# Attention with a routed expert layer on one core: another order in the prologue, slots' weights two at a time, all pieces of q and k stored between the gathers

## The reference

```python
xn  = layernorm(x)                              # no scale, no shift
q, k, v = xn @ Wq + bq, xn @ Wk + bk, xn @ Wv + bv     # 16 heads of 16
q, k = rope(q), rope(k)
att = softmax(q k^T / 4, causal) v @ Wo + bo    # per batch and head
# routed experts: 64, each token goes to 6; F = 176
w, ids = top_k(softmax(xn @ gate_w^T), 6);  w = w / (sum(w) + 1e-20)
routed = sum over the six: w * (silu(xn @ Wg_e) * (xn @ Wu_e)) @ Wd_e
shared = (silu(xn @ Sg) * (xn @ Su)) @ Sd       # width 2 * 176
out = x + att + routed + shared
```

## Time and profile before

| what | us |
|---|---|
| median of three runs | 740.29 |
| the three runs | 731.63, 740.29, 740.82 |
| the profiled execution | 730.91 |
| its span | 729.0 |
| around the span | 1.9 |
| prologue to the last tile's logits | 0 to 34 |
| projections and routing | 34 to 74 |
| shared experts | 74 to 154 |
| routed experts | 155 to 514 |
| attention | 514 to 729 |

### The profile page before, as it was taken

The page is one execution under the profiler, slowest core; times in us unless marked ns, Lnnn a source line. Parts: engine busy times, 40 slices in busy tenths (PEclk is TensorE's granted clock), DMA queues, the critical chain, the costliest instruction groups (busy, mean ns, idle before and its releaser), DMA issues.

```text
span 729.0 us, 18953 instructions
## 1 busy us (share of the span) xinstructions
PE 676.1 (93%) x4876; PEld 405.8 (56%) x4877; DVE 435.6 (60%) x1184; ACT 319.3 (44%) x830; POOL 360.6 (49%) x376
## 2 busy tenths in 40 slices
PE   7999999989999999999999999998888798899857
PEld 4745777755555555555555555554445465455534
DVE  4588999975454454454455555543557656667534
ACT  2653222224444444444444444443556445556332
POOL 3000000258587677586687878466155434554450
PEclk9999999999999999999999999999999979999879
DMA  8420001236877968869776785469865545554221
GB/s 253 136 62 0 1 1 34 85 120 198 265 218 223 308 200 270 289 199 298 233 222 210 213 255 174 100 140 326 277 195 175 166 136 170 167 173 122 75 73 44
DMA packets 77120, 124.02 MB, mean 170 GB/s; under 512 B 11047, under 2 KB 51176, under 8 KB 77080
## 3 DMA queue, kind: packets, MB, share of 16 engines
q1 hardware_dynamic: 41206, 59.89, 27.4%
q0 software_dynamic: 15872, 46.16, 21.7%
q10 hardware_dynamic: 20002, 17.47, 7.2%
HBM read 85.73 MB, written 37.75 MB: 169 GB/s over the span
## 4 chain that ended last, share of the span: by engine, by line
PE 82%; another core or an unknown queue 4%; DVE 4%; issue 3%; DMA 2%; ACT 2%; SPq 1%; DVEq 1%; ACTq 0%
PE pair L1152 22%; PE pair L1194 13%; PE pair L1138 5%; PE pair L1125 5%; PE bank L1161 4%; PE pair L1028 4%; PE pair L1176 4%; PE bank L1257 3%; PE pair L1221 3%; PE pair L1239 2%; PE bank L1289 2%; PE pair L1231 2%; PE pair L1033 2%; PE pair L1213 2%
## 5 line engine op out<-in xcount | busy, mean ns | idle before, releaser
L433 POOL DMA_INDIRECT lower<-xn_rows,idx_all x128 | 135.9, 1061 | 215.6 <-DVE idx_all L823 121.7
L1152 PE MATMUL pair<-space,work 128*64 (+1 forms) x768 | 167.0, 467 | 11.1 <-issue 4.8
L1194 PE MATMUL pair<-lower,work 88*64 x512 | 121.8, 379 | 1.3 <-ACT work L615 0.7
L833 DVE TENSOR_TENSOR work<-work,pair 128x176 f32<-128x176 f32 x160 | 53.8, 337 | 105.7 <-ACT work L600 79.7
L1152 PEld LDWEIGHTS pair<-space,work 128*64 128x64 f32 x768 | 67.5, 137 | 83.8 <-issue 52.5
L600 ACT ACTIVATE work<-pair 128x176 f32<-128x176 f32 x160 | 50.9, 318 | 125.2 <-PE pair L1152 66.0
L1194 PEld LDWEIGHTS pair<-lower,work 88*64 88x64 f32 x512 | 69.5, 136 | 48.2 <-issue 8.3
L635 ACT ACTIVATE pT<-pair 128x768 f32<-128x768 f32 x64 | 51.9, 811 | 88.5 <-PE pair L1243 63.1
L1152 PE MATMUL pair<-wqkv_sb,work 128*64 128x352 f32 x256 | 89.4, 472 | 0.0
L914 DVE TENSOR_REDUCE negm<-pair 128x2 f32<-128x256 f32 (+1 forms) x128 | 64.9, 551 | 30.9 <-PE pair L1221 26.6
L607 ACT ACTIVATE lower<-pair 128x256 f32<-128x256 f32 x128 | 49.2, 384 | 75.4 <-PE pair L1194 75.2
(11 more groups left out here) (186 smaller groups left out, 1217.7 us busy)
## 6 DMA issues: line engine op xcount, KB each, us to landing
space<-wgu SPq DMA_DIRECT2D x66, 352.0 KB
y_rows<-lower ACTq DMA_DIRECT2D x128, 128.0 KB
qk_all<-qk_rows SPq DMA_DIRECT2D x64, 256.0 KB
lower<-wdn SPq DMA_DIRECT2D x66, 176.0 KB
qk_rows<-space POOLq DMA_DIRECT2D x32, 256.0 KB
qk_rows<-qk_all POOLq DMA_DIRECT2D x32, 256.0 KB
x_all<-x SPq DMA_DIRECT2D x4, 512.0 KB, 7.4
xn_rows<-qk_all SPq DMA_DIRECT2D x16, 128.0 KB, 1.8
```

The source lines that it names most:

```text
L433: po.indirect_dma_start(xg[:, r % XB, :], None, xn_rows[:, :], bass.IndirectOffsetOnAxis(idx_all[:, r:r + 1], 0)).then_inc(xg_in[r % XB], 16)
L833: dve.tensor_tensor(hid[:, u % 2], sg[:, u % 2], pair[u % 2][:, F:2 * F], ALU.mult).then_inc(hid_ok, 1)
L1152: last = pe.matmul(pair[u % 2][strip, 0:2 * F], xgT[u][:, c, strip], n, start=c == 0, stop=c == EC - 1, skip_group_check=True)
L1194: last = pe.matmul(pair[u % 2][strip, 512:512 + E], hT[:, u % 2, c, strip], n, start=c == 0, stop=c == 1, skip_group_check=True)
```

## The change

- SP loads x in five transfers (2, 2, 4, 4 and 4 tiles), then Wv, Wq and Wk, then the constants that ACT issued before; ACT keeps only the identity and the router's weights.
- LayerNorm goes in groups of 2, 2, 4 and 8 tiles. ACT does a square root of a constant first (so that its table is loaded), and takes the second group's root at t = 2, the third's at t = 4, the fourth's at t = 8.
- A step of `slot_weights` is two fused instructions over 128 x 64 (equal, times, with the sum written by `accum_out`) in place of one over 128 x 384. There are still 48 steps; the last four now stand at i = 28 in place of i = 30.
- DVE's `beside(i)` does `up_copy` before the list and the weights.
- PE loads its first four expert numbers beside shared tile i = 24, not after the loop.
- POOL: all eight pieces are rotated and stored between gathers 5 and 111: 136 steps. Nothing stands behind the last gather.

```diff
+EXPERTS_AT = 24
-WEIGH_AT = sorted([-2] * 2 + 2 * list(range(1, 20, 3)) + 3 * list(range(21, 31)) + [22, 24])
+WEIGH_AT = sorted([-2] * 2 + 2 * list(range(1, 20, 3)) + 4 * list(range(21, 29)))
-LN_GROUPS = ((0, 4), (4, 8), (8, 16))
+LN_GROUPS = ((0, 2), (2, 4), (4, 8), (8, 16))
+X_LOADS = (0, 2, 4, 8, 12, 16)
...
+            for i, (t0, t1) in enumerate(zip(X_LOADS, X_LOADS[1:])):
+                sp.dma_start(x_all[:, t0:t1], xv[:, t0:t1]).then_inc(x_in[i], 16)
             w = wqkv.rearrange("(c p) n -> p c n", p=P)
             sp.dma_start(wqkv_sb[:, :, QK:], w[:, :, QK:]).then_inc(wv_in, 16)
             sp.dma_start(wqkv_sb[:, :, 0:QK], w[:, :, 0:QK]).then_inc(w_in, 16)
+            sp.dma_start(bqk_sb[:], bqk.to_broadcast([P, QK])).then_inc(c_in_act, 16)
...
+            sp.dma_start(iota_f[:], iota).then_inc(c_in_act, 16)
...
-            steps = [(n, k) for n in range(PIECES) for k in range(PIECE_STEPS if n < LATE else ROPE_STEPS)]
+            steps = [(n, k) for n in range(PIECES) for k in range(PIECE_STEPS)]
...
-            for n in range(LATE, PIECES):
-                late(n)
...
+            act.wait_ge(ones_ok, 1)
+            act.activation(col[0:NE, 0:1], ones_c[:], ACT.Sqrt)
             root(0)
             for t in range(NT + 1):
+                if t == 2:
+                    root(1)
                 if t in V_AFTER:
                     if t == 4:
-                        root(1)
+                        root(2)
...
-                if step == 0:
-                    i = dve.tensor_tensor(part, key[:, t].unsqueeze(1).to_broadcast([P, TOPK, NE]),
-                                          top[:, t, 0:TOPK].unsqueeze(2).to_broadcast([P, TOPK, NE]), ALU.is_equal)
-                elif step == 1:
-                    i = dve.tensor_tensor(part, part, comb[:, t].unsqueeze(1).to_broadcast([P, TOPK, NE]), ALU.mult)
-                else:
-                    i = dve.tensor_reduce(w6[:, t, 0:TOPK], part, AX.X, ALU.add)
+                for k in range(2 * step, 2 * step + 2):
+                    i = dve.scalar_tensor_tensor(part[:, k], key[:, t], top[:, t, k:k + 1], comb[:, t], ALU.is_equal,
+                                                 ALU.mult, accum_out=w6[:, t, k:k + 1])
...
             def beside(i):
-                list_beside(i)
                 if i + 3 in early[:2]:
                     up_copy(i + 3, (i + 3) % XB)
+                list_beside(i)
...
+                if i == EXPERTS_AT:
+                    for u in range(XB):
+                        load_expert(SHARED_TILES + u, u)
...
-            for u in range(XB):
-                load_expert(SHARED_TILES + u, u)
```

More of the change, by code:

```diff
@@ L148, in build @@
         ring = sb("ring", [P, RING, 2, S], F32R)
-        assert STAGE * 2 * S == NT * E and LATE == BUFS and BUFS * 2 * SPAN_T <= NT * E and NT * E - (WB - FIRST) * GU >= GU + DN
+        assert STAGE * 2 * S == NT * E and BUFS * 2 * SPAN_T <= NT * E and NT * E - (WB - FIRST) * GU >= GU + DN
         assert NT * NE <= (WB - FIRST) * DN and WB * DN + 2 * XB * E == RING * 2 * S
@@ L241, in build @@
         listed_at = bank[0][:, 0:RT]
-        x_in = [sem(f"x_in{i}") for i in range(4)]
+        x_in = [sem(f"x_in{i}") for i in range(len(X_LOADS) - 1)]
         w_in = sem("w_in"); wv_in = sem("wv_in"); wr_in = sem("wr_in"); c_in = sem("c_in"); c_in_act = sem("c_in_act"); id_in = sem("id_in")
@@ L341, in _ @@
             sp.dma_start(wqkv_sb[:, :, 0:QK], w[:, :, 0:QK]).then_inc(w_in, 16)
+            sp.dma_start(bqk_sb[:], bqk.to_broadcast([P, QK])).then_inc(c_in_act, 16)
+            for c in range(EC):
+                sp.dma_start(bv_t[:, c:c + 1], bv[:, c * P:(c + 1) * P].rearrange("o p -> p o")).then_inc(c_in_act, 16)
+            sp.dma_start(bo_sb[:], bo).then_inc(c_in_act, 16)
+            sp.dma_start(rope_sb[:], rope).then_inc(c_in_act, 16)
+            sp.dma_start(tri_f[:], tri).then_inc(c_in_act, 16)
+            sp.dma_start(mask_f[:], mask).then_inc(c_in_act, 16)
+            sp.dma_start(tok_sb[:], tok).then_inc(c_in_act, 16)
+            sp.dma_start(iota_f[:], iota).then_inc(c_in_act, 16)
             sp.dma_start(wo_sb[:], wo.rearrange("(c p) n -> p c n", p=P)).then_inc(c_in, 16)
@@ L486, in _ @@
             assert done == todo
-            def late(n):
-                for k in range(ROPE_STEPS, PIECE_STEPS):
-                    piece(n, k)
-            for n in range(LATE, PIECES):
-                late(n)
             def rows(t, u):
@@ L518, in _ @@
             act.dma_start(wr_sb[:], wr.rearrange("(c p) n -> p c n", p=P)).then_inc(wr_in, 16)
[L519 to L527, removed]
             def xnT_copy(t):
@@ L565, in _ @@
                     if t == 8:
-                        root(2)
+                        root(3)
                     projected(V_AFTER[t][1])
@@ L690, in layernorm @@
                 for t in range(t0, t1):
[L691 removed]
+                    if t in X_LOADS:
+                        dve.wait_ge(x_in[X_LOADS.index(t)], 16)
                     last = dve.bn_stats(stats[:, t], x_all[:, t])
@@ L1099, in list_tokens, with load_expert @@
                 mm.then_inc(listed, 1)
+            expert_reg = [pe.alloc_register(f"expert{u}") for u in range(XB)]
+            def load_expert(i, u):
+                pe.reg_load(expert_reg[u], tile_e[0:1, 0, bass.ds(i, 1)])
             def list_beside(i):
@@ L1107, in list_beside @@
                         x_transpose(SHARED_TILES + k, k)
-            expert_reg = [pe.alloc_register(f"expert{u}") for u in range(XB)]
-            def load_expert(i, u):
-                pe.reg_load(expert_reg[u], tile_e[0:1, 0, bass.ds(i, 1)])
+                if i == EXPERTS_AT:
+                    for u in range(XB):
+                        load_expert(SHARED_TILES + u, u)
             def expert_of(u):
```

5 lines of the change are left out of this document (removed).

## The result

The changed kernel took 751.8 us (median of 14 runs, 740.1 to 763.4); the kernel before, run beside it, 736.7 (14 runs, 727.0 to 744.8). The ratio is 1.0133, 95% interval 1.0095 to 1.0172: slower by 1.3%. Runs of one kernel fall into a faster and a slower group; the ratio compares the faster ones alone (6 of these 14, median 744.0), which is why it is smaller than 751.8 / 736.7. The profiled execution of the changed kernel took 752.1 us (span 750.0); that of before 730.9 (span 729.0). The two profiles lie further apart than the medians, so lines tell here where time went and ratios tell how much.

The account below looks back on a forecast made before the run. PE, 82% of the chain, was taken as the bound. Terms +2.0 + 0 - 0.5 + 4.2 - 2.7 = +3.0 gave 733.9 us on the profiled scale, 739.0 with 5.1 added for the runs' median; range 725 to 752.

Parts of the forecast that it names:

- Pieces stored between the gathers: Routed loop: -3.8 from the last pairs, +4.8 for four more store phases, +3.2 for late gathers; together +4.2 us.
- start of attention: End of loop and start of attention: -2.1 for two faster y stores, -0.6 for the ring's ninth copy; -2.7 us.
- The stores' own terms: Routed loop: four more phases of eight stores at 1.2 each, 4.8; gathers late by 0.4 for each of 8 pieces, 3.2.
- The rest, 3.7: Routed loop before the change: 3.7 us lost to other collisions, such as slowed weight copies on DVE; their number stays.
- with three: Routed loop: a pair with three rope steps takes POOL 6.7 us, after which its gathers are 1.4 late.
- The last pairs' -3.8: Last three routed pairs, beside the 32 late stores: they get back the 3.8 us lost there.
- Prologue: Start of the kernel: first tile's gain hidden by the warm-up, PE waits some 1.9 for tile 2; +2.0 us.
- its upper bound, the low clock: Prologue: TensorE's clock falling to half after the new gap would cost half of 3.4, +1.7 us.
- Slot weights: DVE beside the shared experts: a step of two instructions takes 0.54, saving about 1 us, hidden behind PE; 0.
- Rival 3: DVE falls behind with four slot-weight steps a tile: +4 on the sum, 743.0 us; chance 0.10.
- Hand-over: Where routed experts begin: PE goes on 1.0 sooner, held by gather 5; register loads cost +0.5; sum -0.5 us.
- Rival 2: Routed loop: DMA queues fill up in store phases, 16 pairs at 6.86; +14.8, 750.8 us; chance 0.16.

Follow-up runs that it names:

- s1_spread: The kernel before with all 64 stores spread between the gathers, nothing else; ratio to before 1.0118, loop 338.3 us.
- r1_half_rope: s1_spread with six of nine rope steps of a piece on half their columns, all stores in place (computes another result); ratio to before 1.0030, loop 331.6 us.
- q1_dense: The kernel before with its unchanged 104 steps drawn into 44 pairs in place of 56, no store added; ratio 1.0239 over six runs.
- p1_prologue: The kernel before with the change's LayerNorm groups, loads of x, constants on SP and root's table ahead alone; ratio 1.0005.
- h1_handover: The kernel before with the fused slot weights, up_copy ahead of them and register loads at i = 24 alone; ratio 0.9992.
- l1_late_again: The changed kernel with pieces 4 to 7 stored after the last gather again; ratio to the kernel before 1.0021.
- c1_by_cost: s1_spread with POOL's list paced by cost (rope step 145, store 57) in place of count; ratio to the kernel before 1.0077.
- i1_interleaved: s1_spread with a piece's stores one by one between the next piece's rope steps; ratio to the kernel before 1.0095.
- m1_six: The kernel before with pieces 4 and 5 also stored in the loop and the list over 60 pairs, two steps each; ratio 1.0056.

## Why the prediction was wrong

Predicted were 739.0 us, +3.0 over before; the runs give +9.8 (interval 7.0 to 12.7 on 737).

**Pieces stored between the gathers, +4.2: this step failed.** With the start of attention's -2.7 it made +1.5; s1_spread measured +8.7 (5.4 to 12.1). The stores' own terms were of the right size: 4.8 + 3.2 = 8.0, where r1_half_rope leaves some 7 (of which its waits for gathers are 3.9, not all of it as the prediction's terms had it). Missing was a term behind the sentence "The rest, 3.7, I put down to other collisions, such as weight copies on DVE that take 1.56 us in place of 0.53 while POOL works; the change leaves their number as it is". The number of copies that a rope step holds did stay nearly as it was (33, then 41 in the changed kernel, 44 in s1_spread). Their price didn't: they stood later, where PE has to wait for them. PE's wait before up-matmuls grew by 5.9 in s1_spread, 2.6 came before down-matmuls, and 6.7 us of the loop went away when POOL's steps were made shorter. The prediction had both halves in hand, the slow copy in the earlier trace rows and the 6.7 us of a pair "with three", but let the late POOL delay only its gathers, by 1.4, and never asked what DVE does in that time. r1_half_rope shows it with the stores held in place; q1_dense shows it with no store added.

The last pairs' -3.8 was right, and rather small: from the up-matmuls of the 61st pair to those of the 64th the kernel before took 19.8 us, s1_spread 15.4, and to the last down-matmul 5.1 came back in all. The sum then closes. The six kernels with the old list took 324.3 on average in the loop; 338.3 - 324.3 - 5.1 is +8.9 for s1_spread, where +8.7 was measured (give or take 3.4), and 331.6 - 324.3 - 5.1 is +2.2 for r1_half_rope, where +0.3% is +2.2.

**Prologue, +2.0.** The wait was foreseen (1.9 at 13.5; 1.65 at 14.2), and so was its upper bound, the low clock. Three profiles with this prologue reach the first shared up-matmul at 78.26, 77.59 and 76.45; the nine with the old one at 73.65 to 76.97, mean 74.5. So in the profiles it costs near 2.9, of which p1_prologue's interval (-2.6 to +3.2 us) allows all and shows nothing; the +4 expected of p1_prologue lies outside it. The constants landed in time. With the constants off ACT the warm-up began 0.5 us sooner on average (3.74 to 4.19 in five profiles, 4.17 to 4.78 in nine), which the prediction did not expect. And the old prologue isn't safe from this clock either: in q1_dense the warm-up ended early, PE stood 1.82 us for the first tile, and tile 4 came at 22.69 in place of 19.83; in s1_spread it came at 21.50. The warm-up hides the LayerNorm only where it is slow: it took 5.87 to 7.38 us.

**Slot weights, 0.** Right. DVE's timeline in the changed kernel:

```profile
155.38 0.28 DVE L848 SCALAR_TENSOR_TENSOR space<-space,top 128x64 f32<-128x64 f32 x1
155.58 0.08 DVE L848 DVE_READ_ACCUMULATOR space<-space,top 128x1 f32 x1
155.70 0.29 DVE L848 SCALAR_TENSOR_TENSOR space<-space,top 128x64 f32<-128x64 f32 x1
```

The instruction takes 0.28, its separate read of the accumulator 0.08, mostly overlapped: a step of two about 0.53, where 0.54 was taken. The second instruction that the Trainium skill (VectorE: DVE Perf Modes, Two Vector instructions with no wait between them) announced is there, and small. Rival 3 had no ground.

**Hand-over, -0.5.** Right in size, but not in its reason. From the first shared up-matmul to the eighth pair's transposes: before 114.9, changed kernel 114.3, h1_handover 114.1, l1_late_again 114.4. h1_handover stood 2.7 us ahead at the third pair and went on there without waiting for gather 5, which the prediction had put in the way: its issue ended at 154.22 and PE used its rows from 157.50, sooner than the 5 us that were taken as the least. It lost 2.3 in the next two pairs, where POOL's steps held DVE's copies:

```profile
157.50 2.20 DVE L872 COPY wqkv_sb<-space 128x704 f32 x1 [0.38 <-issue]
```

```profile
160.00 0.42 PE L1161 MATMUL bank<-id_f,work 128*88 128x128 f32 x2 [1.62 <-DVE work L834]
```

In l1_late_again one pair took 9.33 us there. The first copy started in the last half microsecond of a gather (159.50 to 160.45), and the rope step right behind that gather (160.47 to 161.74) held it on; the second copy was held by the next rope step:

```profile
159.93 2.21 DVE L872 COPY wqkv_sb<-space 128x704 f32 x1 [0.38 <-issue]
...
162.30 1.33 DVE L872 COPY space<-space 128x704 f32 x1
```

**Start of attention, -2.7.** The stores of y take 0.34 again in place of 1.38 and 1.41. The ring's ninth copy waits 0.17 for its load in place of 5.53, but ACT's next copy then waits 5.44 for PE:

```profile
528.31 4.27 ACT L639 ACTIVATE ring<-qk_all 128x512 fp32r<-128x512 f32 x8 [0.41 <-ACT lower L603]
532.76 1.30 ACT L639 ACTIVATE ring<-qk_all 128x512 fp32r<-128x512 f32 x2 [0.17 <-DMA qk_all<-qk_rows]
539.50 0.38 ACT L649 ACTIVATE mT<-bank 128x256 fp32r<-128x256 f32 x1 [5.44 <-PE bank L1268]
```

so what was a wait became another, as foreseen. From the last down-matmul the first exponential came after 14.9 us in the changed kernel and after 15.8 to 21.6 in the seven kernels with 32 late stores, the fifth after 29.1 and after 27.0 to 30.9: nothing that lasts. By that, and by the sum above, which leaves nothing for this part but the 0.8 that came back between the 64th pair's up-matmuls and the last down-matmul, -2.7 was too much, as far as single profiles tell.

**Rivals.** The median of 751.8 lies inside the stated range only by its edge; by the ratio the change is +9.8, three times the forecast. Rival 2 gave the nearest time (750.8), and part of its mechanism is real (c1_by_cost). But late gathers are only a fifth of PE's added idle time in the changed kernel (2.8 of 14.0); the price came out near for the wrong reason.

## What to carry to other kernels

When a list of steps is packed into the gaps of a loop, look at the fullest gap, not at the mean: 2.43 steps a round means three in some rounds, and the question is what runs on the other engines just after the gap. Write down, for each engine that the busy one can hold up (DVE by POOL here), at what point of the round its instruction starts; a wait that was nobody's in a calm round can be PE's when the neighbour is 1.3 us late. A stalled instruction seen in the old profile has no fixed price: ask not only how often the change will make it occur, but how late in the round it will then stand.

## What the runs showed that was not expected

The last stage is the largest source of spread. From the 64th pair's transposes to the end i1_interleaved took 227.5 us and m1_six 245.1, at mean granted clocks of 0.93 and 0.85. Only 2.2 us of the difference lie before the last down-matmul, where m1_six has its late stores; behind it the code is the same:

```profile
502.58:730.10 227.52, 198.14 (x1719) 115.35 (x1717) 134.88 (x344) 111.18 (x205) 91.78 (x96) 0.93 0.45 135
```

```profile
498.20:743.30 245.10, 214.89 (x1717) 124.17 (x1717) 134.11 (x341) 110.57 (x204) 91.50 (x96) 0.85 0.45 135
```

PE is busy 16.8 us longer for nearly the same number of matmuls. A single profile can therefore be off by more than the whole effect of this change, and i1_interleaved's profile (span 730.1) looks like a kernel as fast as before, though its twelve runs say 0.95% slower.

What stays open: what DVE waited for ahead of the held `down_copy`, and why gathers come late beside three and four stores. The stores stand ahead of them in POOL's own queue, and all DMA engines are busy; no run here moved the stores to another queue to tell the two apart.
